# Expert down products from high and low halves, with ScalarE and VectorE looping expert by expert

## The reference, cut to what matters

```python
logits = x @ gate_w.T;  probs = softmax(logits)
vals, idx = top_k(probs, 2);  vals = vals / vals.sum(-1)
w = zeros(bs, 16).at[rows, idx].set(vals)
gate_out = (x @ g.T).reshape(bs, 16, 112)
up_out   = (x @ u.T).reshape(bs, 16, 112)
h = silu(gate_out) * up_out
out = einsum('bei,hei,be->bh', h, d.reshape(1024, 16, 112), w)
```

## Time and profile before

| | |
|---|---|
| median of 3 runs | 1355.69 us |
| time of the profiled execution | 1356.5 us |
| its span, first to last instruction | 1354.8 us |
| TensorE busy over the span | 1239.7 us (92%) |
| VectorE, ScalarE, GpSimd busy | 783.7, 513.5, 573.0 us |
| mean granted TensorE clock | 0.971 of full speed |
| the `experts` stage's tiles, first to last down product | 602.60 to 837.53 us |

### The profile page before, as it was taken

The page is one execution under the profiler, slowest core; times in us unless marked ns, Lnnn a source line. Parts: engine busy times, 40 slices in busy tenths (PEclk is TensorE's granted clock), DMA queues, the critical chain, the costliest instruction groups (busy, mean ns, idle before and its releaser), DMA issues. The chain is left out here.

```text
span 1354.8 us, 20940 instructions
## 1 busy us (share of the span) xinstructions
PE 1239.7 (92%) x6442; PEld 846.7 (62%) x6442; DVE 783.7 (58%) x2026; ACT 513.5 (38%) x939; POOL 573.0 (42%) x931
## 2 busy tenths in 40 slices
PE   4799999999878999999999998999999999968886
PEld 2354544445435954458888786988888898635443
DVE  3889999998963680015433333444554443369885
ACT  2555545454423400023322222232222322168894
POOL 5667877777642001013221222523212231068884
PEclk8999999999988899999999999999999999879998
DMA  5211212302004502227778874535333331131111
GB/s 197 92 64 32 93 62 96 138 31 109 0 1 149 224 1 84 70 85 246 265 240 283 273 233 161 187 94 128 114 103 124 96 101 54 62 70 47 62 62 78
DMA packets 52481, 156.25 MB, mean 115 GB/s; under 512 B 5952, under 2 KB 16192, under 8 KB 52288
## 3 DMA queue, kind: packets, MB, share of 16 engines
q1 hardware_dynamic: 39152, 113.46, 23.6%
q0 software_dynamic: 13264, 41.95, 10.8%
HBM read 112.93 MB, written 45.61 MB: 117 GB/s over the span
## 5 line engine op out<-in xcount | busy, mean ns | idle before, releaser
L1210 PEld LDWEIGHTS ex_bank<-ex_xT,ex_gu 128*112 128x112 f32 x1248 | 140.4, 177 | 24.3 <-issue 23.3
L1210 PE MATMUL ex_bank<-ex_xT,ex_gu 128*112 128x128 f32 x1248 | 143.6, 273 | 2.0 <-issue 1.0
L44 PE MATMUL xa_bank<-fT_high,M_hi 128*128 128x256 f32 x512 | 144.0, 281 | 0.0
L46 PE MATMUL xa_bank<-fT_high,M_lo 128*128 128x256 f32 x512 | 143.0, 279 | 0.0
L45 PE MATMUL xa_bank<-fT_low,M_hi 128*128 128x256 f32 x512 | 142.9, 279 | 0.0
L52 PE MATMUL la_bank<-la_osum,la_tab 128*128 128x512 f32 x256 | 120.8, 617 | 24.1 <-POOL la_osum L291 23.7
L291 POOL TENSOR_TENSOR la_osum<-la_oprod 128x512 f32<-128x512 f32 x64 | 80.1, 1273 | 73.7 <-DVE la_oprod L479 73.7
L1074 POOL TENSOR_TENSOR ex_small<-listed,ex_small 128x1 int32<-128x1 int32 x42 | 15.4, 368 | 223.7 <-DVE Wk L1152 223.5
L52 PEld LDWEIGHTS la_bank<-la_osum,la_tab 128*128 128x128 f32 x256 | 47.7, 196 | 86.4 <-issue 48.6
L44 PEld LDWEIGHTS xa_bank<-fT_high,M_hi 128*128 128x128 f32 x512 | 96.7, 189 | 0.3
L46 PEld LDWEIGHTS xa_bank<-fT_high,M_lo 128*128 128x128 f32 x512 | 96.7, 189 | 0.0
(11 more groups left out here) (284 smaller groups left out, 2853.4 us busy)
## 6 DMA issues: line engine op xcount, KB each, us to landing
produced<-Wk SPq DMA_DIRECT2D x39, 512.0 KB
ex_gu<-in_gate_up SPq DMA_DIRECT2D x16, 896.0 KB
X<-in_x SPq DMA_DIRECT2D x8, 1024.0 KB, 7.4
la_v_raw<-in_ctx SPq DMA_DIRECT2D x16, 512.0 KB, 4.0
produced<-la_zeros SPq DMA_DIRECT2D x16, 512.0 KB, 4.7
normal<-rt_xn SPq DMA_DIRECT2D x16, 512.0 KB, 5.4
fT<-in_ctx_T SPq DMA_DIRECT2D x8, 1024.0 KB, 5.7
xa_f<-in_ctx SPq DMA_DIRECT2D x8, 1024.0 KB, 4.8
```

The lines of the kernel that those rows point to most:

```text
L44: pe.matmul(out, a[0], b[0], start=first, stop=False)
L46: return pe.matmul(out, a[1], b[0], start=False, stop=last)
L1210: m = pe.matmul(bank[half][0:INTER, 0:P], gu[:, slot, at:at + INTER], xT[:, k, :], start=(k == 0), stop=(k == KD - 1))
```

## The change

The down product becomes three float32r products, as in the next stage, and its halves are made inside `experts`:

- `dn_high` and `dn_low`: at the start of each expert ScalarE copies its 112x1024 down weights into `dn_hi` (float32r, one buffer), and VectorE subtracts, `dn - dn_hi`, into `dn_lo`, which lies on the slot of `dn` itself.
- `h_hi`, `hT`, `h_lo`: for each tile VectorE writes the product of silu and up twice, once as float32r and once as float32, and subtracts.
- TensorE does four products of 512 columns with `h_hi`, waits for `hT_lo`, and does two with `h_lo`; before the first it also waits for `dn_lo` of the expert.
- ScalarE and VectorE loop expert by expert, as TensorE does, and read the bounds for it. The pieces of work for the next stage are done once for each of the first twelve experts, ahead of the expert's tiles, instead of once in each of the first twelve tiles.
- SyncE waits for `dn_lo` ahead of loading the weights of a later expert.

```diff
@@ -990,7 +990,7 @@
                 merged_product(pe, bank[n % 4][:], W, n).then_inc(s["m_pe"], 1)
 
 
-def experts(nc, gate_up, down, normal, listed, produced, first_tile, W, M32, M, features_T, fT, fT_parts):
+def experts(nc, gate_up, down, normal, listed, produced, first_tile, W, M32, M, features_T, fT, fT_parts, halves):
 
     with ExitStack() as ctx:
         held = ctx.enter_context(phase_semaphores(nc))
@@ -1005,7 +1005,9 @@
         SLOTS = 3
         merged_bank = [6, 7, 4, 5]
         gu = sb("gu", [P, SLOTS, KD * UP_COLS])
+        at = -(-nc.sbuf_base // 32) * 32
         dn = sb("dn", [INTER, SLOTS, D])
+        dn_low = nc.alloc_sbuf_tensor_at("ex_dn_low", [INTER, SLOTS, D], F32R, offset=at)
         small = sb("small", [P, 4], I32)
         current, nought, spare = small[:, 0:2], small[:, 2:3], small[:, 3:4]
         xr = sb("xr", [P, 2, D])
@@ -1014,8 +1016,12 @@
         hT = sb("hT", [INTER, P])
         y, xs = W[1][:, 0, :], W[1][:, 1, :]
         ident = W[1][:, 6, 0:P]
+        h_hi, h_lo, dn_hi = (tensor[:] for tensor in halves)
+
+        def dn_lo(slot):
+            return dn_low[:, slot, :]
         names = """one consts current rows_ready rows_held turned xT_act xT_dve gate_done up_half up_done silu_done hT_ready down_done
-                   m_pe m_out m_hi fT_in fT_hi y_act y_dve y_st all_stored""".split()
+                   m_pe m_out m_hi fT_in fT_hi y_act y_dve y_st all_stored dn_hi dn_lo hT_whole hT_lo""".split()
         s = {n: sem(n) for n in names}
         arrived = [sem(f"arrived{i}") for i in range(2)]
         w_in = [sem(f"w_in{i}") for i in range(SLOTS)]
@@ -1052,6 +1058,7 @@
                     sp.dma_start(produced[bass.ds(row, P), :], y[:]).then_inc(s["y_st"], 16)
                 if e + SLOTS < EXPERTS:
 
+                    sp.wait_ge(s["dn_lo"], e + 1)
                     load(e + SLOTS)
             sp.wait_ge(s["all_stored"], 1)
 
@@ -1112,27 +1119,37 @@
                 act.wait_ge(s["m_pe"], n - EARLY + 1)
                 act.activation(merged_part(M32, n), bank[merged_bank[n % 4]][:], ACT.Copy).then_inc(s["m_out"], 1)
             rows_out(0)
-            total = act.value_load(first_tile[0:1, EXPERTS:EXPERTS + 1], min_val=1, max_val=MAX_TILES)
+            def beside(e):
+
+                if e < KD:
+                    part = merged_columns(e)
+                    act.activation(M[0][part], M32[part], ACT.Copy).then_inc(s["m_hi"], 1)
+                elif e < BESIDE:
+                    part = features_part(e - KD)
+                    act.wait_ge(s["fT_in"], 16)
+                    act.activation(fT_parts[0][part], fT[part], ACT.Copy).then_inc(s["fT_hi"], 1)
+
+            def down_high(e):
+
+                act.wait_ge(w_in[e % SLOTS], 32 * (e // SLOTS + 1))
+                at_least(act, s["dn_lo"], e)
+                act.activation(dn_hi, dn[:, e % SLOTS, :], ACT.Copy).then_inc(s["dn_hi"], 1)
 
             def tile(g):
                 act.wait_ge(s["gate_done"], g + 1)
                 act.activation(sg[:], bank[0][0:INTER, 0:P], ACT.Silu).then_inc(s["silu_done"], 1)
                 rows_out(g + 1)
-                if isinstance(g, int) and g < KD:
-                    part = merged_columns(g)
-                    act.activation(M[0][part], M32[part], ACT.Copy).then_inc(s["m_hi"], 1)
-                elif isinstance(g, int):
-                    part = features_part(g - KD)
-                    act.wait_ge(s["fT_in"], 16)
-                    act.activation(fT_parts[0][part], fT[part], ACT.Copy).then_inc(s["fT_hi"], 1)
                 act.wait_ge(s["down_done"], g + 1)
                 act.wait_ge(s["y_st"], 16 * g + 16)
                 act.activation(y[:, 0:512], bank[4][:], ACT.Copy).then_inc(s["y_act"], 1)
             act.wait_ge(s["m_out"], 2 * KD - EARLY)
-            for g in range(BESIDE):
-                tile(g)
-            with act.Fori(BESIDE, total) as g:
-                tile(g)
+            for e in range(EXPERTS):
+                down_high(e)
+                beside(e)
+                lo, hi = bounds(act, e)
+                with act.Fori(lo, hi) as g:
+                    tile(g)
+            total = act.value_load(first_tile[0:1, EXPERTS:EXPERTS + 1], min_val=1, max_val=MAX_TILES)
             act.wait_ge(s["y_st"], total * 16 + 16)
             act.activation(sg[:, 0:1], ident[0:INTER, 0:1], ACT.Copy).then_inc(s["all_stored"], 1)
 
@@ -1155,30 +1172,41 @@
             hold(0)
             rows_out(0)
             hold(1)
-            total = dve.value_load(first_tile[0:1, EXPERTS:EXPERTS + 1], min_val=1, max_val=MAX_TILES)
+            def beside(e):
+
+                if e < KD:
+                    part = merged_columns(e)
+                    dve.wait_ge(s["m_hi"], e + 1)
+                    dve.tensor_tensor(M[1][part], M32[part], M[0][part].bitcast(F32), ALU.subtract)
+                elif e < BESIDE:
+                    part = features_part(e - KD)
+                    dve.wait_ge(s["fT_hi"], e - KD + 1)
+                    dve.tensor_tensor(fT_parts[1][part], fT[part], fT_parts[0][part].bitcast(F32), ALU.subtract)
+
+            def down_low(e):
+
+                dve.wait_ge(s["dn_hi"], e + 1)
+                dve.tensor_tensor(dn_lo(e % SLOTS), dn[:, e % SLOTS, :], dn_hi.bitcast(F32), ALU.subtract).then_inc(s["dn_lo"], 1)
 
             def tile(g):
                 dve.wait_ge(s["silu_done"], g + 1)
                 dve.wait_ge(s["up_done"], g + 1)
-                dve.tensor_tensor(hT[:], sg[:], bank[1][0:INTER, 0:P], ALU.mult).then_inc(s["hT_ready"], 1)
+                dve.tensor_tensor(h_hi, sg[:], bank[1][0:INTER, 0:P], ALU.mult).then_inc(s["hT_ready"], 1)
+                dve.tensor_tensor(hT[:], sg[:], bank[1][0:INTER, 0:P], ALU.mult).then_inc(s["hT_whole"], 1)
+                dve.wait_ge(s["hT_whole"], g + 1)
+                dve.tensor_tensor(h_lo, hT[:], h_hi.bitcast(F32), ALU.subtract).then_inc(s["hT_lo"], 1)
                 rows_out(g + 1)
                 hold(g + 2)
-                if isinstance(g, int) and g < KD:
-                    part = merged_columns(g)
-                    dve.wait_ge(s["m_hi"], g + 1)
-                    dve.tensor_tensor(M[1][part], M32[part], M[0][part].bitcast(F32), ALU.subtract)
-                elif isinstance(g, int):
-                    part = features_part(g - KD)
-                    dve.wait_ge(s["fT_hi"], g - KD + 1)
-                    dve.tensor_tensor(fT_parts[1][part], fT[part], fT_parts[0][part].bitcast(F32), ALU.subtract)
                 dve.wait_ge(s["down_done"], g + 1)
 
                 dve.wait_ge(s["y_act"], g + 2)
                 dve.tensor_copy(y[:, 512:1024], bank[5][:]).then_inc(s["y_dve"], 1)
-            for g in range(BESIDE):
-                tile(g)
-            with dve.Fori(BESIDE, total) as g:
-                tile(g)
+            for e in range(EXPERTS):
+                down_low(e)
+                beside(e)
+                lo, hi = bounds(dve, e)
+                with dve.Fori(lo, hi) as g:
+                    tile(g)
 
         @block.tensor
         def _(pe):
@@ -1216,8 +1244,14 @@
 
                     pe.wait_ge(s["y_act"], g + 1)
                     pe.wait_ge(s["y_dve"], g + 1)
+                    pe.wait_ge(s["dn_lo"], e + 1)
                     for i in range(2):
-                        m = pe.matmul(bank[4 + i][:], hT[:], dn[:, slot, i * 512:(i + 1) * 512], start=True, stop=True)
+                        half = slice(i * 512, (i + 1) * 512)
+                        pe.matmul(bank[4 + i][:], h_hi, dn_hi[:, half], start=True, stop=False)
+                        pe.matmul(bank[4 + i][:], h_hi, dn_lo(slot)[:, half], start=False, stop=False)
+                    pe.wait_ge(s["hT_lo"], g + 1)
+                    for i in range(2):
+                        m = pe.matmul(bank[4 + i][:], h_lo, dn_hi[:, i * 512:(i + 1) * 512], start=False, stop=True)
                     m.then_inc(s["down_done"], 1)
 
 
@@ -1910,11 +1944,13 @@
                 def quarter(name, i, dt=F32):
 
                     return nc.alloc_sbuf_tensor_at(name, [P, KD, L], dt, offset=at + i * 2 * D * 4)
+                halves = [nc.alloc_sbuf_tensor_at(name, [INTER, cols], F32R, offset=at + first * 4)
+                          for name, first, cols in (("h_high", 6 * D + P, P), ("h_low", 6 * D + 2 * P, P), ("down_high", 7 * D, D))]
                 xn = W[1][:, 0:2, :]
                 fT, fT_parts, xT = quarter("fT", 1), [quarter("fT_high", 2, F32R), quarter("fT_low", 1, F32R)], quarter("xT", 3)
                 route(nc, gw, X, running, normal, listed, slots, weights, first_tile, Wk, W, M32, bk, bq,
                       shift, key_bias, constant)
-                experts(nc, gate_up, down, normal, listed, produced, first_tile, W, M32, [M_hi, M_lo], ctx_T, fT, fT_parts)
+                experts(nc, gate_up, down, normal, listed, produced, first_tile, W, M32, [M_hi, M_lo], ctx_T, fT, fT_parts, halves)
```

## The result

The changed kernel takes 1367.7 us, median of four runs (1367.3 to 1372.61); the kernel before took 1355.72 us, median of four (1354.49 to 1356.04). The ratio is 1.0098, 95% interval 1.0075 to 1.0122, 13 us slower; the two medians lie 12 us apart. The profiled execution of after took 1367.68 us. The forecast was 1359.2 us: the right side and inside the range of 1349 to 1370 us, but 8.5 us too low and above the range that I gave the forecast itself, 1356 to 1365 us.

A forecast was written before the change was run, and what follows sets the result against it. TensorE was taken to bound the experts stage. Changes of expert +17.9 us, allowance +0.8, products -15.2 gave +3.5 us on the profiled 1356.5 us, 1360.0; the median before being 0.8 lower, 1359.2 us, range 1349 to 1370.

The forecast's parts named there:

- The products: Down products: six float32r products at 0.222 us, 1.33 us a tile, gaining 0.39 us each, 15.2 us over 39 tiles.
- `h` in halves, the pieces, expert 0: VectorE's extra h work hidden with 0.5 us to spare; moving the next stage's pieces and expert 0's halves gain or cost nothing.
- From ScalarE's copy to the next down products: At changes of expert, halves, pieces and bounds take 4.95 us (experts 1-7), 4.55 (8-11), 3.95 (12-15).
- Lateness: ScalarE's last-tile copies wait for stores: 0.8 us at expert 3, on average 2.0 us at experts 7 to 11, added at changes.
- lump of 0.8 us: Allowance in the stage for later stores, time given back at changes, and late h: 0.8 us (0 to 5).
- TensorE's own path: At changes of expert, bounds read behind the h_lo wait make gate products 0.87 us late, 5.1 us from end to start.
- Together, from end to start: All 15 changes of expert, last products to next: 84.4 us against 66.5 before, 17.9 us more.
- The clock: TensorE's clock in the stage: new gaps of 1 to 2.5 us cause no change of level.
- (1): Rival: changes of expert stay cheap as stores catch up, TensorE's path decides; net -5.2 us, 1350.5 us; chance 0.26.
- (2): Rival: stores become late by 2.0 us at every expert, changes 98.7 us; net +17.0 us, 1372.7 us; chance 0.18.
- (3): Rival: VectorE's subtractions hold up GpSimd's gathers at 15 changes; +18 us on the forecast, 1377 us; chance 0.04.
- (4): Rival: six float32r products cost 0.43 us each like float32 records; 49 us above the forecast, 1408 us; chance 0.02.

The follow-up runs named there:

- e1: Kernel before with the six float32r products and halves of h, but one high half of the down weights for all products: 1353.64 us, ratio 1.0011.
- e2: Kernel before, float32 products kept, with ScalarE and VectorE looping expert by expert, pieces and bounds at each, no halves: 1362.11 us, ratio 1.0073.
- e3: Changed kernel with ScalarE's and VectorE's loop bounds read once, ahead of the stage: 1360.19 us, ratio 1.0076 to the kernel before.
- e8: e7 with GpSimd issuing a gather only after the store of the tile just finished is issued: 1356.01 us, ratio 1.0026 to the kernel before.
- e10: e9 with the store in two halves, each behind its own copy, each copy waiting only for its half: 1335.55 us, ratio 0.9867 to the kernel before.
- e5: e1 with TensorE's loop bounds read once, ahead of the stage and of the merged products: 1364.45 us, ratio 1.0089 to the kernel before.
- e9: e8 with TensorE's bounds read two at a time between merged products: 1342.87 us, ratio 0.9925 to the kernel before.
- e7: Changed kernel with halves and pieces made inside each expert's first tile, two high buffers, all bounds read ahead: 1359.58 us, ratio 1.0052 to the kernel before.

## Why the prediction was right, and where its numbers were off

The side was right for the reason given: the products gain, and the changes of expert lose more, because the by-work of ScalarE and VectorE stands between two tiles instead of inside one. e1 and e2 show both parts. The forecast for the stage was +3.5 us and it measured +16.5; outside the stage lie -5.7 us that I hadn't forecast, so that the total looks better than its terms is luck. Term by term:

**The products.** Forecast 1.33 us a tile, measured 1.40: the gain is 0.33 us and not 0.39, 2.3 us over 38 periods. 512 columns of float32r take 0.233 us from start to start, twice the 0.117 us of 256. I took part of the 0.117 us for a cost of each product; hardly anything of it is. It was the upper bound of my own range. The Trainium skill's rule for an isolated product (TensorE: Matmul & The Clock Gate, Back-to-back issue gap), 0.216 us by my estimate, isn't borne out for these products, which start 0.233 us apart.

**`h` in halves, the pieces, expert 0.** As forecast: `h_low` 0.7 us ahead of its products, and the first down product earlier than before, not later.

**From ScalarE's copy to the next down products.** The sequence came as written, and in its first instance to 0.1 us: 4.95 us forecast, 5.03 measured. Over experts 1 to 7 it is 5.33 us on average, over 8 to 11 4.74 (forecast 4.55), over 12 to 15 4.1 (3.95). The sum is 72.6 us against 68.7, 3.9 more; what varies most between experts is VectorE's reading of bounds, which leaves it idle for 0.20 to 1.76 us ahead of `h`, and the longest way is 5.92 us in all. e3 takes the reading away and the idle time ahead of the down products falls by 8.8 us.

**Lateness.** This term failed most. I carried the lateness of rows 7 over to experts 4 to 12, 11.9 us; it is 19.3 us, and begins with expert 0: the copy at 609.01 is late by 1.9 us (the products ended at 607.06), where the earlier trace rows has 0.04 us. I had put what shorter periods do to stores into a lump of 0.8 us. My reading of before was wrong in one place as well: I wrote that elsewhere a last copy is late by 0.4 us or less, but expert 14's last one (822.17) is late by 1.0 us, which changes nothing in the sum:

```profile
822.17 0.60 ACT L1130 ACTIVATE Wk<-ex_bank 128x512 f32<-128x512 f32 x1 [2.54 <-DMA produced<-Wk]
```

What shorter periods do could be worked out: copy 0.60, VectorE's copy 0.69, issue 0.18, landing 4.7 us are 6.2 us from one ScalarE copy to the next, more than a period of 5.76 us and about one of 6.09. At a change of expert the lateness is on the path, since the halves start behind the copy. e8 (gather behind the store) and e10 (store in two) show that it is the store: with both, the late time at changes is 10.9 us and none of it costs TensorE anything.

**TensorE's own path.** I had the gate products start 2.20 us after the down products at a change (0.35 + 1.85), 0.87 us late. They start 2.27 us after them on average, against 1.49 us inside experts, so 0.78 us late, of which the profile shows 0.64 us as idle time. I used this path as a floor for the changes of experts 1 to 3 and 13 to 15, 3.9 us; it was never needed, as the other path was later everywhere. Where the other path is short it decides alone, as e1 shows.

Together, from end to start: 84.4 us forecast, 92.5 us measured (72.6 us and 19.9 us of copies after the end of products), against 66.5 us before: 8.1 of the 13 us that the stage's forecast lacked. The rest: 2.3 us at the 15 changes, as the products last 1.64 us with their latency and not 1.49, 1.4 us in the 23 periods inside, and 1.6 us of the clock, less the lump of 0.8 us.

**The clock.** I counted no change of level. There is one: from 749.6 to 753.0 us the granted clock is 0.50, which is the lower level (1.2 GHz), after TensorE had been idle 1.98 us ahead of the products at 748.58. That period takes 7.41 us instead of 5.77, so 1.6 us. e1 has such a spell after a gap of 1.11 us. The gap of 1.94 us ahead of 614.04 is followed by products at the full pace, so why these two and not the others stays open.

**Rivals.** (1) needed under 5.45 us from end to start; it is 6.2 us. It fell. (2), stores late at every expert, 98.7 us: the truth, 92.5, is a little past halfway from the forecast to this rival. Its mechanism is there at nearly all changes, with 1.3 us on average and not 2.0. For the stage as a whole it gave +17.0 us, which the measured +16.5 is much nearer to than to the forecast's +3.5, though by other terms: the products and the clock make up part of it. (3) GpSimd: VectorE's copy of gathered rows, which would show a late gather, has no idle time ahead of it:

```profile
L1169 DVE COPY Wk<-ex_xr 128x1024 f32 x39 | 26.6, 683 | 0.0
```

(4) fell with 0.233 us a product. Of the conditions set ahead, the periods inside experts average 5.84 us, over my 5.8, but the usual one is 5.76; nearly all of the excess is the clock's 1.6 us in one tile.

## What to carry to other kernels

When a stage's bound engine gets shorter work, list every loop that ran beside it with little to spare (here the store's loop, 6.2 us beside 6.09) and put its length beside the new period before summing the gain. Work for the next group of tiles belongs inside a tile, behind what that tile's successor waits for, and not at the boundary where nothing is queued; e10 differs from the change only in where by-work, readings and transfers stand, and turns +1.0% into -1.3%. A loop's bounds are a load with a latency: here it cost nothing where products were queued, and most behind a wait (e1) or ahead of the bound engine's work (e5).

## What the runs showed of the hardware that I had not expected

- float32r with 512 columns, 0.233 us from start to start at the full clock: twice the price of 256 columns (0.117 us), with hardly a cost per product.
- A reading of a loop bound on TensorE costs 0.66 us (11.2 us for 17) when nothing is queued, and leaves no idle time between queued products (e5, e9).
- The order of two issues 0.8 us apart, gather and store, changes ScalarE's waits for stores from 75.8 to 113.2 us over 39 tiles (e8, e7).
